# Counting the positions of a pair's tokens with thirteen matrix products in place of twenty

## The reference

```python
logits = -dist2 + jnp.einsum('bld,ed->ble', x, rw) + rb      # 16 experts
topv, topi = jax.lax.top_k(logits, TOP_K)                    # 4 of 16 for every token
w = jax.nn.softmax(topv, axis=-1)
hidden = jax.nn.gelu(jnp.einsum('bld,efd->blef', x, w1) + b1, approximate=False)
exp_out = jnp.einsum('blef,edf->bled', hidden, w2) + b2
sel = jnp.take_along_axis(exp_out, topi[..., None], axis=2)
fused = jnp.sum(w[..., None] * sel, axis=2)
```

## Time and profile before

| what | value |
|---|---|
| median of 3 runs | 385.86 us (383.79, 385.86 and 552.42) |
| the profiled execution's own time | 384.52 us |
| its span, first to last instruction | 382.7 us |
| mean granted TensorE clock | 0.861 |
| PE busy, weight loads busy | 297.7 us, 269.9 us |
| DVE, ACT, POOL busy | 186.7, 214.6, 154.7 us |

### The profile page before, as it was taken

How to read it: one execution, slowest core, us unless ns; L and a number is a source line. 1 busy time by engine, 2 the same in 40 slices (tenths; PEclk the granted TensorE clock), 3 DMA queues, 4 the chain that set the end, 5 groups by cost and what they waited for, 6 DMA issues and landing times.

```text
span 382.7 us, 11689 instructions
## 1 busy us (share of the span) xinstructions
PE 297.7 (78%) x3548; PEld 269.9 (71%) x3549; DVE 186.7 (49%) x817; ACT 214.6 (56%) x763; POOL 154.7 (40%) x167
## 2 busy tenths in 40 slices
PE   4986988585756756262779837999999989999893
PEld 4975877373745545142779736999999989999662
DVE  4065378053443527134446644666555555665163
ACT  2455388244351706213347533788888878898345
POOL 4015000705243342552654645466555645533300
PEclk9996699778685959575859958899999999999998
DMA  7999100101000010120212212122222212210195
GB/s 235 233 380 408 72 3 3 54 9 41 22 33 30 24 40 11 54 60 32 68 53 59 63 49 67 51 77 75 69 71 70 69 57 68 64 48 14 29 388 135
DMA packets 25407, 32.44 MB, mean 85 GB/s; under 512 B 4315, under 2 KB 18292, under 8 KB 25104
## 3 DMA queue, kind: packets, MB, share of 16 engines
q1 hardware_dynamic: 20576, 22.38, 19.7%
q0 software_dynamic: 4352, 8.79, 6.7%
q10 hardware_dynamic: 432, 0.67, 0.6%
HBM read 20.84 MB, written 11.50 MB: 85 GB/s over the span
## 4 chain that ended last, share of the span: by engine, by line
PE 65%; issue 11%; another core or an unknown queue 8%; ACT 7%; DVE 5%; DMA 3%; DVEq 0%; ACTq 0%; POOLq 0%; SPq 0%; POOL 0%
PE bank L760 15%; PE bank L781 14%; PE bank L561 4%; PE bank L576 4%; PE bank L755 4%; ACT hs L1573 3%; PE bank L745 3%; PE bank L771 2%; PE bank L622 2%; PE bank L845 2%; PE bank L532 2%; PE bank L548 1%; PE bank L603 1%; ACT shared L1736 1%
## 5 line engine op out<-in xcount | busy, mean ns | idle before, releaser
L1897 POOL DMA_INDIRECT yrows<-shared,idi x72 | 79.5, 1104 | 70.5 <-issue 40.0
L1829 POOL DMA_INDIRECT xrows<-rows_all,sli x64 | 61.8, 965 | 109.3 <-issue 48.3
L1736 ACT ACTIVATE shared<-bank,shared 128x128 f32<-128x128 f32 x256 | 73.3, 371 | 31.7 <-PE bank L760 22.2
L781 PE MATMUL bank<-w2s,shared 128*128 x512 | 72.0, 286 | 9.2 <-ACT shared L1736 9.2
L760 PE MATMUL bank<-shared 128*128 128x128 f32 x512 | 73.6, 291 | 0.1
L781 PEld LDWEIGHTS bank<-w2s,shared 128*128 128x128 f32 x512 | 66.2, 202 | 10.1 <-issue 10.1
L760 PEld LDWEIGHTS bank<-shared 128*128 128x128 f32 x512 | 67.9, 207 | 0.5 <-issue 0.3
L1386 DVE COPY shared<-w1s 128x644 f32 x64 | 32.1, 501 | 28.1 <-issue 27.8
L1722 ACT ACTIVATE shared<-bank 128x128 f32<-128x128 f32 x72 | 21.0, 292 | 22.2 <-remote 16.2
L745 PE MATMUL bank<-cst,shared 128*128 128x128 f32 x72 | 21.3, 295 | 14.4 <-ACT shared L1722 9.3
L1755 ACT ACTIVATE shared<-shared,idg 128x128 f32<-128x128 f32 x72 | 30.2, 422 | 1.5 <-DVE shared L1396 1.4
(11 more groups left out here) (235 smaller groups left out, 518.8 us busy)
## 6 DMA issues: line engine op xcount, KB each, us to landing
shared<-xrows SPq DMA_DIRECT2D x64, 70.0 KB
w1s<-in_w1T SPq DMA_DIRECT2D x1, 4128.0 KB, 23.3
w2s<-in_w2T SPq DMA_DIRECT2D x1, 4096.0 KB, 23.6
w1s<-yrows SPq DMA_DIRECT2D x8, 512.0 KB, 6.8
yrows<-shared,idi POOLq DMA_INDIRECT x72
xrows<-zrow SPq DMA_DIRECT2D x1, 1120.0 KB, 12.2
w1s<-in_b SPq DMA_DIRECT2D x1, 1024.0 KB, 22.5
xrows<-rows_all,sli POOLq DMA_INDIRECT x64
```

The lines of the kernel that those rows point to most:

```text
L781: m = mm(out_bank(u), hT[u][:, f * P:(f + 1) * P], w2s[:, bass.ds(ex, 1), f, :], start=(f == 0), stop=(f == FB - 1))
L1736: m = act(hT[u][:, f * P:(f + 1) * P], hidden_bank(u)[:, f * P:(f + 1) * P], ACT.Gelu, bias=w[:, F + f:F + f + 1])
L1829: po.indirect_dma_start(out=xrows, out_offset=bass.IndirectOffsetOnAxis(ap=sli[:, g, k:k + 1], axis=0), in_=rows_all[:, g, :], in_offset=N ...
L1897: po.indirect_dma_start(out=yrows, out_offset=bass.IndirectOffsetOnAxis(ap=idi[r][:, 0:1], axis=0), in_=yw[r][:, :], in_offset=None, bound ...
```

## The change

The twenty products of 16 columns become thirteen. The choices of half 0 are multiplied by `ones16` once, with the moving operand read twice (a broadcast), so that one product of 32 columns adds them to the ranks of half 1 and to the total at once (4 products). The ranks within both halves come from one product of 2 x 16 columns for each choice, apart from choice 0, which takes two products of 16 columns (5 products). The choices of half 1 are added to the total alone (4 products). The order of the results, the semaphore and everything on the other engines stay.

```diff
-                for q in range(NC):
-                    for k in range(TOPK):
-                        mm(late[:, 288 + q * E:288 + (q + 1) * E], before[:, :], oh[m_ % 2][:, q, k, :], start=(k == 0),
-                           stop=(q == 0 and k == TOPK - 1))
+                both = oh[m_ % 2]
                 for k in range(TOPK):
-                    mm(late[:, 288 + E:288 + 2 * E], ones16[:, :], oh[m_ % 2][:, 0, k, :], start=False, stop=(k == TOPK - 1))
-                for q in range(NC):
-                    for k in range(TOPK):
-                        m = mm(late[:, 320:320 + E], ones16[:, :], oh[m_ % 2][:, q, k, :], start=(q == 0 and k == 0),
-                               stop=(q == 1 and k == TOPK - 1))
+                    mm(late[:, 288 + E:288 + 3 * E].rearrange("p (c e) -> p c e", c=2), ones16[:, :],
+                       both[:, 0:1, k, :].broadcast_to([P, 2, E]), start=(k == 0), stop=False, skip_group_check=True)
+                mm(late[:, 288:288 + E], before[:, :], both[:, 0, 0, :], start=False, stop=False, skip_group_check=True)
+                mm(late[:, 288 + E:288 + 2 * E], before[:, :], both[:, 1, 0, :], start=False, stop=False, skip_group_check=True)
+                for k in range(1, TOPK):
+                    mm(late[:, 288:288 + 2 * E].rearrange("p (q e) -> p q e", q=NC), before[:, :], both[:, :, k, :], start=False,
+                       stop=(k == TOPK - 1), skip_group_check=True)
+                for k in range(TOPK):
+                    m = mm(late[:, 320:320 + E], ones16[:, :], both[:, 1, k, :], start=False, stop=(k == TOPK - 1),
+                           skip_group_check=True)
                 m.then_inc(s1["pos_mm"], 1)
```

## The result

Over 19 runs of each, the changed kernel has a median of 382.43 us (378.60 to 386.62), the kernel before 384.29 us (381.06 to 386.61 apart from its one run of 552.42). The ratio is 0.9924, with an interval of 0.9898 to 0.995. By this first sample the gain is more than the 0.5 us that I had forecast. The ratio leaves out runs that are more than 1.5% above the fastest of their kernel; here these were five of the changed kernel and none of the other, so beside each ratio I also give the difference of the means over all runs (those disturbed like the 552.42 excepted) with its standard error. For this sample it is -1.5 ± 0.6 us.

What follows compares the result with a forecast made beforehand. PE was taken as the chain, its crawls in steps 4 to 7 ending with POOL's trains of sends. Terms summed to 1.4 us unhalved or 0.20 halved; 0.5 us was taken, giving 384.2 us from a mean of 384.7, range 381.8 to 387.4.

Steps and rivals of the forecast that it cites:

- The crawl follows the train: Steps 4 to 7: PE's slow, gapped stretch ends about 1.4 us behind POOL's last indirect send, whatever the number of products.
- paid by the piece: Rival: crawl ends after a certain amount of work, each removed product worth 0.27 to 0.29 us; 376.5 or 380.5 us; chance 0.1.
- Fewer products left at the resumption: Sign, steps 4 to 7: some 23 to 26 products of line 576 left when PE resumes, in place of 29 to 32.
- DVE's `pos` still waits some 7 us: Sign, steps 4 to 7: DVE's wait for the positions' count ends with the train and stays some 7 us.
- 0.25 us a step at the resumption, halved each time: positions(1) to (4): 6 fewer products left at 0.043 us each; 1.0 us in all, 0.24 if the low clock halves each gain.
- Positions(0) at nothing: Step 3: seven products fewer save 0.21 us, which goes into PE's 0.67 us wait for ACT's `yiT`, so 0.
- (5) at nothing: positions(5) runs at 161 us in the open while DVE masks scores until 163.2, so its gain is 0.
- Positions(6) and (7): Both lie on the path to the next train: seven products fewer give 0.20 and 0.18 us, perhaps halved by the low clock.
- The width at nothing: Seven products of 32 columns in place of 16 cost 0; other end about 0.05 us a pair.
- The eighth send joins the train: Rival, steps 5 to 7: `y_intra`'s count seen earlier, train 1.26 us longer; 387.8 us, about 386 with clock's share; chance 0.1.
- PE's "issue" moves to line 576: Sign: PE's idle time without known releaser moves from line 681 to line 576 and doesn't shrink.
- the lower end: The sum with gains halved by the low clock at every resumption, 0.20 us at the end, against 1.4 us without any halving.

Runs made afterwards that it cites:

- the dummies in the crawl: Kernel before with 28 unread products more at the head of positions(1) to positions(4), inside each crawl: 389.98 us, ratio 1.0082, difference +6.1 ± 0.8 us.
- four products: Four products in place of the kernel before's twenty in every pair, using one DVE comparison: 380.40 us, ratio 0.9977; second sample, chip without crawls, 310.80 us, 0.9886.
- second trace: Trace from the changed kernel run once more, unedited, beside the kernel before on the same chip: 382.58 us, ratio 0.9987, difference -0.7 ± 0.7 us.
- 28 products more: Kernel before with 28 products more at the head of project(2s) in steps 4 to 7, just behind each resumption: 388.78 us, ratio 1.0142, +5.6 ± 0.9 us.
- the four samples together: Changed kernel against the kernel before, two samples on chips with crawls, two without: ratios 0.9924, 0.9987, 0.9921, 0.9937; pooled difference -0.7 ± 0.3 us.
- a split train: Kernel before with the fifth send of pairs 0 to 4 held for the positions' count, on chips without crawls: 312.32 us, 0.9977; again 311.48 us, 0.9972.

## Why the prediction was right and wrong

**The crawl follows the train: right.** Shown by the dummies in the crawl (1.4 us behind the last send, 31 us of expected cost not there) and by four products, where 16 fewer left it at 1.41. That rules out the rival *paid by the piece*. In the first trace of the changed kernel the distance was 1.49 to 1.54, up to 0.14 longer than before. In its second trace and in that with thirteen in pairs 1 to 4 it is 1.39 to 1.44, so this is not of the change. That the sends cause the crawl is argued from this timing and not shown: on the other chips the same sends go out without one.

**Fewer products left at the resumption: right.** They are 24, 27 and 26 in steps 5 to 7, where there were 29, 31 and 32; in the second trace they are 23, 21 and 22. Over steps 5 to 7 of three traces with thirteen and eight with twenty the means are 23.6 and 30.4, about the seven that were taken out; I had said 6, and 23 to 26 left. **DVE's `pos` still waits some 7 us: right**, 7.03 us. Step 4 ended differently in the first trace: its eighth send started 0.88 us behind the end of the seventh in place of 0.30, and PE resumed 0.94 us behind it, with 9 left in place of 13. In the second trace that send is on time.

**0.25 us a step at the resumption, halved each time: the size fits, and can't be told from nothing.** Thirteen in pairs 1 to 4 gave -0.1 ± 0.5 us, the stretch over three steps -0.3 ± 0.3, and that between the resumptions of steps 5 and 7 -0.1 ± 0.1. All are with the 0.24 of the halved sum, and the last rules out the one without a halving. But the reason that I gave, a slow time of fixed length in which work counts half, failed: behind the four resumptions the kernel before has 14.9 us of it in one trace and 19.6 in the other, and with 28 products more it is 23.9. These cost 0.040 us each by the trace and 0.050 ± 0.008 by the runs, more than the 0.028 of such a product in the open. So a small gain may be lost altogether, and a larger load may cost more than itself.

**Positions(0) at nothing: wrong, and (5) at nothing: right.** Positions(0) became shorter by 0.18 us, and PE's wait for `yiT` is 0.69 us in place of 0.67. So the gain did not go into the wait: `yiT` itself came earlier by it. From the first product of positions(0) to that of line 603 the six traces with thirteen there have 6.39 to 6.42 us, the twelve with twenty 6.56 to 6.58, and POOL's first train starts 9.63 to 9.65 us behind the same product in place of 9.80 to 9.83. The term is 0.17 us, near the 0.21 that I had without the cover. The run with pair 0 alone, +0.5 ± 0.6 us, can't see it. From positions(5) to (6) it is 20.1 to 20.4 us with thirteen and 20.1 to 20.2 with twenty: no gain, as forecast.

**Positions(6) and (7): right in their trace.** 0.19 and 0.17 us less, where I had 0.20 and 0.18; from the start of positions(6) to the next train it is 2.43 us in place of 2.61. Their runs alone, -0.6 ± 0.6 and +0.4 ± 0.6, can't see such amounts.

**The width at nothing: right within what can be seen.** The thirteen, seven of them wide, took 0.41 us in step 3, 0.032 each, against 0.030. The 0.05 us a pair at the other end of my range is as near as zero.

**The eighth send joins the train: did not happen.** It went out at 117.02, behind the resumption at 116.64, in step 6, and likewise in steps 5 and 7.

**PE's "issue" moves to line 576: half wrong.** It left lines 675 to 681 (12.9 us before, 10.1 in their successors), but that of line 576 went from 6.5 to 6.1, while its busy time went from 18.9 to 23.5 us. Its products have 344 ns each, as before (345), but more of them stand apart and fewer overlap, and so it is their busy time that grows and not the gaps. The chain's share of "issue" stayed at 11%.

**The number: the step that failed** is the sum, "I take 0.5 us, nearer to the lower end, since the rows of the clock are that way in all four steps". Its term for positions(0), "The gain goes into that wait: 0", was wrong: it measured 0.17 us. And I took the clock's schedule of one execution for that of all, in the lower end and in the spread around it. But neither reaches the size that was measured. The first sample is 1.5 ± 0.6 us faster by its means, and 2.9 us by the ratio, which lies wholly beyond 0.5. The runs put in the sum's place: the terms that were read in traces are 0.17, 0.19 and 0.17 us at positions(0), (6) and (7) and between nothing and some 0.3 in the crawls, so 0.5 to 0.8 us; the four samples together give 0.7 ± 0.3 us; and the same unchanged kernel moves by 3.2 us between two traces and by 1.0 ± 0.5 us between two samples. Where the rest of the first sample, about 1 us, comes from is open. The clock that comes back some 3 us earlier or later at single places moves one trace by 1.4 us at each, but that it did so more often with the change is not shown. Against it speaks that the run with the new form in pairs 0, 5, 6 and 7 has the same mean clock as the kernel before beside it, 0.8625 and 0.8615 over all runs, and is 1.8 us faster all the same.

What else stays open: whether that run's 1.8 ± 0.7 us, of which the single places show nothing, is more than chance; whether the changed kernel's runs spread more for a reason (2.0 to 2.9 us of standard deviation in its samples, 1.2 to 1.9 with the kernel before); and whether a split train helps on a chip that crawls, which was not tried.

## What to carry to other kernels

Ask of every product that you remove where the time goes that it frees: under a stall that ends with something else it only changes the queue behind the stall. In front of a wait look at what the other engine waits for itself before you write down a zero: here ACT's `yiT` came earlier together with PE, the wait kept its 0.7 us, and the gain was kept as well. Where TensorE's granted clock falls and comes back within a kernel, two profiles differ by more than a small edit is worth, so compare a stretch that both traces pass at full clock, and run the unchanged kernel against itself before you believe a microsecond. Cut both traces at the same products, too: here the first two differed by 3.0 us ahead of the first changed instruction. When the number of small products is what you pay for, look for one operation on another engine that makes most of them needless: a single comparison of 0.19 us a pair replaced sixteen products of twenty, where rearranging them saved seven.

## What was not expected of the hardware

- The same kernel takes 383 us on one chip and 312 us on another. All the difference that I followed is PE's crawl under POOL's indirect sends: steps of 20.6 us with it, of 10.6 without, at the same pace of the sends. Why one chip has it and another not is open.
- 28 small products, by their number 0.8 us of work, cost 1.1 us a step behind a crawl in the trace and 1.4 ± 0.2 in the runs. PE was then at 1.2 GHz for 23.9 us behind the four resumptions, where the traces without them have 14.9 to 22.5.
- Between two traces of an unchanged kernel, PE had 106 or 96 us at 1.2 GHz in the span, and the span differed by 3.2 us. In the one stretch from positions(6) to (7) the clock's return makes 24.9 to 25.6 or 26.7 to 27.2 us in fourteen traces, whichever form of the products runs there.
